# FFN gates in a Mamba and SwiGLU kernel: three Silus in a stretch of their own on ScalarE in place of Tanh and a VectorE operation for each

## What is computed

```python
h = x * rsqrt(mean(x * x) + 1e-05) * norm_w
xs, res = split(h @ in_proj_w.T)                  # 256 channels each
u = silu(causal_conv4(xs) + conv_b)
delta, Bm, Cm = split(u @ x_proj_w.T)             # 64, 16, 16
delta = softplus(delta @ dt_proj_w.T + dt_proj_b)
# state[d, n] = exp(delta * A) * state + delta * u * Bm ; y = sum_n state * Cm, over 512 tokens
y = (y + u * D) * silu(res)
x = layernorm(x + y @ out_proj_w.T + x)
gate, up = x @ wg.T, x @ wu.T                     # 384 hidden units, weights are int / 127
x = layernorm(x + (silu(gate) * up) @ wd.T)
```

## Time and profile before

| | |
|---|---|
| timed runs | 622.06, 623.67, 625.15 us; median 623.67 |
| profiled execution | 623.23 us; span 621.3 us |
| busy | TensorE 442.2 us (71%), VectorE 536.4 (86%), ScalarE 354.9 (57%), GpSimd 388.2 (62%) |
| chain that ended last | VectorE 37%, TensorE 22%, issue 17%, ScalarE 10%, GpSimd 8% |
| TensorE's granted clock, mean | 0.798 of full speed |

### The profile page before, as it was taken

One profiled execution on the slowest core, in us unless ns is written; L12 is line 12 of the kernel. 1 busy time (PEld: TensorE's weight loads), 2 busy tenths in 40 slices (PEclk: granted clock), 3 DMA queues, 4 the chain that ended last, 5 costly groups with the idle time before them and its releaser, 6 DMA issues.

```text
span 621.3 us, 5665 instructions
## 1 busy us (share of the span) xinstructions
PE 442.2 (71%) x1469; PEld 175.7 (28%) x1469; DVE 536.4 (86%) x584; ACT 354.9 (57%) x592; POOL 388.2 (62%) x168
## 2 busy tenths in 40 slices
PE   3963957778859777786958875986958784667443
PEld 2411311323314223322414232422323240312232
DVE  4536999799999899989998899999999999999823
ACT  2264677458653975567753965387556955344322
POOL 4504667854975857865884777676695587575000
PEclk9955968787789879788969879887979887757767
DMA  8038005410246006510443005600533024600000
GB/s 210 0 77 195 1 0 120 102 49 1 36 100 152 2 1 136 125 27 0 90 100 97 0 4 131 152 0 0 135 81 71 0 52 95 141 1 0 17 1 17
DMA packets 27359, 39.10 MB, mean 63 GB/s; under 512 B 3816, under 2 KB 10056, under 8 KB 27344
## 3 DMA queue, kind: packets, MB, share of 16 engines
q1 hardware_dynamic: 25424, 38.51, 27.1%
q10 hardware_dynamic: 1920, 0.42, 0.4%
HBM read 3.27 MB, written 2.10 MB: 9 GB/s over the span
## 4 chain that ended last, share of the span: by engine, by line
DVE 37%; PE 22%; issue 17%; ACT 10%; POOL 8%; SPq 3%; DMA 2%; DVEq 1%; ACTq 0%; POOLq 0%
DVE state L783 18%; DVE weighted L792 11%; POOL prod L649 6%; PE c_ps L386 4%; PE y_ps L397 4%; PE dense_ps L417 3%; SPq L315 3%; ACT decay_ps L504 2%; PE dense_ps L446 2%; PE dense_ps L419 2%; PE dense_ps L452 1%; DMA du_rep<-z_wm 1%; ACT L504 1%; ACT x L515 1%; ACT L539 1%
## 5 line engine op out<-in xcount | busy, mean ns | idle before, releaser
L649 POOL TENSOR_TENSOR prod<-du_rep,b_rep 128x2048 f32<-128x2048 f32 x63 | 284.8, 4530 | 64.7 <-DVE state L783 32.3
L783 DVE TENSOR_TENSOR_SCAN state<-decay_ps,prod 128x512 f32<-128x512 f32 x256 | 299.3, 1207 | 23.0 <-ACT decay_ps L504 10.1
L504 ACT ACTIVATE decay_ps<-delta_rep,a_neg 128x512 f32<-128x512 f32 x256 | 172.2, 686 | 78.6 <-DVE state L783 75.7
L386 PE MATMUL c_ps<-xd,pick 96*128 96x512 f32 x128 | 92.9, 816 | 81.3 <-DVE weighted L792 81.2
L792 DVE TENSOR_TENSOR weighted<-state,c_ps 128x2048 f32<-128x2048 f32 x64 | 146.4, 2287 | 2.7 <-DVE state L783 0.6
L397 PE MATMUL y_ps<-weighted,gather 128*32 128x512 f32 x512 | 93.6, 813 | 5.6 <-DVE weighted L792 5.6
L669 POOL TENSOR_TENSOR rs<-ve,powm 128x4 f32<-128x4 f32 x16 | 16.2, 1012 | 108.0 <-ACT nm L510 108.0
L417 PE MATMUL dense_ps<-h_t,tap_t 128*128 128x512 f32 x128 | 65.3, 658 | 11.8 <-ACT h_t L534 11.8
L386 PEld LDWEIGHTS c_ps<-xd,pick 96*128 96x128 f32 x128 | 27.0, 239 | 115.8 <-DVE weighted L792 104.5
L509 ACT ACTIVATE ve<-mv 128x4 f32<-128x4 f32 x16 | 3.3, 205 | 71.7 <-DVE mv L818 45.9
L417 PEld LDWEIGHTS dense_ps<-h_t,tap_t 128*128 128x128 f32 x128 | 25.4, 209 | 48.3 <-issue 40.1
(11 more groups left out here) (109 smaller groups left out, 538.0 us busy)
## 6 DMA issues: line engine op xcount, KB each, us to landing
delta_rep<-z_ln SPq DMA_DIRECT2D x64, 256.0 KB, 4.7
du_rep<-z_wm SPq DMA_DIRECT2D x64, 256.0 KB, 4.8
out_dram<-y_out SPq DMA_DIRECT2D x8, 256.0 KB, 4.5
state<-L_attn_in_proj_w_in ACTq DMA_DIRECT2D x1, 256.0 KB, 4.2
x_all<-L_attn_x_in SPq DMA_DIRECT2D x1, 256.0 KB, 4.7
weighted<-L_ffn_w_gate_in SPq DMA_DIRECT2D x1, 192.0 KB, 10.6
weighted<-L_ffn_w_up_in SPq DMA_DIRECT2D x1, 192.0 KB, 4.7
weighted<-L_ffn_w_down_in SPq DMA_DIRECT2D x1, 192.0 KB, 5.1
```

The source lines that it names most:

```text
L386: mm(c_ps[:, :], pick[:, CHUNKS + quad % CHUNKS, :], xd[it.now][:, :], start=True, stop=True).then_inc(c_ready, 1)
L504: A(decay_ps[n % DECAYS][:, :], delta_rep[:, h, c, :], ACT.Exp, scale=a_neg[:, col:col + 1]).then_inc(decay_ready, 1)
L649: TT(prod[quad % 2][:, :, :], du_rep[:, h, :, :], b, ALU.mult).then_inc(prod_ready, 1)
L783: dve.tensor_tensor_scan(state[:, n % BLOCKS, :], decay_ps[n % DECAYS][:, :], prod[n // BLOCKS % 2][:, n % BLOCKS, :], 0.0, ALU.mult, ALU. ...
```

## The change

The three Tanhs on ScalarE and the three scalar_tensor_tensors on VectorE go. ScalarE makes the three Silus at step 18, in a loop, directly from PSUM into g_act. z_w and z_wm move from steps 18 and 19 to 19 and 20. TensorE makes the three gates first and the up products behind them, in another order of banks; VectorE multiplies by up at steps 20, 21 and 22 instead of 20, 21 and 23.

```diff
-    SILU2 = WSCALE * WSCALE * WSCALE / 2
+    WSCALE2 = WSCALE * WSCALE
-        g_th = sb("g_th", [P, 2, T])
-        g_th_ready = sem("g_th_ready")
-                ["C", "S", "gate0", "up0", "gate1", "up1", "gate2"],
+                ["C", "S", "gate0", "gate1", "gate2", "up0", "up1"],
-                "gate0": 1, "up0": 2, "gate1": 0, "up1": 1, "gate2": 2, "up2": 0, "b0": 1, "b1": 2,
+                "gate0": 1, "gate1": 2, "gate2": 0, "up0": 1, "up1": 2, "up2": 0, "b0": 1, "b1": 2,
# ScalarE
-                    if step == 18 and it.k0 > -1:
+                    if step == 19 and it.k0 > -1:
                         it.wait(act, z_step, 4, 1, 3)
                         A(z_w[:, :, :], z_e[:, :, :], ACT.Copy, bias=1.0).then_inc(z_step, 1)
-                    if step == 19 and it.k0 > -1:
+                    if step == 20 and it.k0 > -1:
                         it.wait(act, du_in[1], 16 * BLOCKS, 0, 16 * BLOCKS)
                         it.wait(act, z_step, 4, 1, 4)
                         A(z_wm[:, :, :], z_w[:, :, :], ACT.Copy, bias=-1.0).then_inc(wm_ready, 1)
-                    for b, at in enumerate((18, 19, 21)):
-                        if step == at:
+                    if step == 18:
+                        for b in range(HID):
                             it.wait_full(act, f"gate{b}")
-                            A(g_th[:, b % 2, :], it.ps(f"gate{b}")[:, :], ACT.Tanh, scale=WSCALE / 2
-                              ).then_inc(g_th_ready, 1)
+                            it.take(A(g_act[:, b, :], it.ps(f"gate{b}")[:, :], ACT.Silu, scale=WSCALE), f"gate{b}")
# VectorE
-                    for b, (at, then) in enumerate(((19, 20), (20, 21), (22, 23))):
-                        if step == then:
+                    for b, at in enumerate((20, 21, 22)):
+                        if step == at:
                             it.wait_full(dve, f"up{b}")
                             it.wait_taken(dve, f"gate{b}")
                             it.take(TT(g_act[:, b, :], g_act[:, b, :], it.ps(f"up{b}")[:, :], ALU.mult), f"up{b}")
-                    for b, (at, then) in enumerate(((19, 20), (20, 21), (22, 23))):
-                        if step == at:
-                            it.wait(dve, g_th_ready, HID, -1, b + 1)
-                            it.take(STT(out=g_act[:, b, :], in0=g_th[:, b % 2, :], scalar=1.0,
-                                        in1=it.ps(f"gate{b}")[:, :], op0=ALU.add, op1=ALU.mult), f"gate{b}")
-                                    scalar=SILU2, in1=x1[:, 2 * n:2 * n + 2, :],
+                                    scalar=WSCALE2, in1=x1[:, 2 * n:2 * n + 2, :],
```

## The result

The changed kernel takes 639.36 us (median of four, 633.16 to 642.41), the kernel before beside it 624.30: a ratio of 1.023, 95% interval 1.0145 to 1.0324. It is slower, as forecast, but by 15 us and not by 9; 639.36 lies 1.4 us above the range. A second set of six times gave 641.73 (ratio 1.022, 1.017 to 1.027). The ten times fall in two groups: four between 633.2 and 637.1 and six between 641.6 and 643.4. Three of the ten, 633.2 to 634.3 us, lie beside the forecast of 632.5; six lie above the 638 us of the slowest rival but D.

What follows compares the result with a forecast made beforehand. Batch ends were set by when GpSimd can start the next multiply(0), through soften(0) and DMA replication. soften(0) +16.0, hidden -4.0, proj wait -1.75, iteration 7 -0.6, iteration 8 -0.7: about +9, forecast 632.5 us, range 626.5 to 638.

Steps and rivals of the forecast that it cites:

- D: Rival: each table switch costs a drain as well, +15 us on top, 647 us; chance 0.02.
- The chain through z_wm, soften and replication: Late z_wm delays GpSimd's error, multiply(6), soften(0), then replication and the next batch's multiply(0); soften(0) 16.0 us later in all.
- Loads: ScalarE around the gates: 15 more table loads of 1.28 us, the first nearly hidden by the gate0 wait, the second paid.
- The delay of z_wm: ScalarE's z_wm ends 4 to 4.7 us later, making soften(0) 2.25 us later at fast clock, 3.5 us at slow.
- Iterations 1 and 4 are of this sort, 2, 3, 5 and 6 of the first: Gate stretches: two iterations at TensorE's slow clock (soften(0) +3.5 us each), four at the fast clock (+2.25 us each).
- 12.0 less 1.75: Iterations 1 to 6: soften(0) 16.0 us later, 4.0 hidden, leaves 12.0; iteration 4's PE wait for proj gives back 1.75.
- rival C: Slow clock in all gate stretches: 6 x 3.5 - 4.0 - 1.75 - 0.7 = +14.5, 638 us; chance 0.10.
- -0.6 and -0.7: Gains from removed VectorE operations in iteration 7 (0 to -1.3, taken -0.6) and the tail, iteration 8 (-0.7 us).
- it gains 0.3 us there, at the fast clock up to 1.3: VectorE at up2's product: waits 1.5 us, saved 1.8; worth nothing in iterations 1 to 6, real in iteration 7.
- A: Rival: VectorE is the bound, so the removed operations count; some -5 us, 618.5 us; chance 0.09.
- B: Rival: effects cancel within 0.5%, fast gates everywhere and early PE waits absorbing half; +1.7, 625.4 us; chance 0.08.
- E: Rival: Silu comes from the active table set, no loads, soften +1.0 all hidden; chance under 0.01, counted in B.

Runs made afterwards that it cites:

- Experiment 3: Kernel before (Tanh, no loads, old TensorE order) with only z_w at step 20 and z_wm behind the third Tanh at step 21; 652.45 us, ratio 1.044.
- 2: Changed kernel with z_w and z_wm both at step 18, ahead of the three Silus; 641.94 us, ratio 1.027.
- 6: Changed kernel with z_w and z_wm at step 18 ahead of the Silus, and eight unread matmuls ahead of the seventh C; 623.07 us, ratio 0.997.
- profile of 635.1 us: First profiled execution of the unaltered changed kernel, named by its span; the execution took 637.07 us, mean TensorE clock 0.814.
- profile of 640.1 us: Profiled execution from the repeat of the unaltered changed kernel, named by its span; the execution took 642.14 us, clock 0.788; the repeat's median was 641.73 us.
- Version 8: Changed kernel with z_w and z_wm at step 18, the three Silus at step 21, up products at steps 22, 22 and 23; 613.27 us, ratio 0.982.
- experiment 4: Changed kernel with eight extra unread matmuls on TensorE between b1 and the seventh list's C; 632.30 us, ratio 1.012.
- experiment 1: Changed kernel with Tanh in place of the three gate Silus, so no table loads around the gates; 632.16 us, ratio 1.010.
- experiment 10: Version 8 with Ln directly behind the Silus, three table loads per iteration instead of four (u's not counted); 620.93 us, ratio 0.993.

## Why the prediction was right in its direction and wrong in its size

**The chain through z_wm, soften and replication: right.** `multiply(0)` waits for du_rep in iterations 1 to 5 of the profile (in iteration 6 for 0.64 us for a scan). From `soften(0)` to the product the six iterations have 4.0 us less than before in all, the 4.0 that the forecast called hidden. Experiment 3 makes the cost with z_wm alone, experiments 2 and 6 take it away (prod's wait 7.7 and 7.8 us).

**Loads: right.** 15 more, 1.28 us each, the first beside the wait for gate0, the second in full, no drain. The Trainium skill (page ScalarE: Activation LUTs, section What ACT_TABLE_LOAD costs) counts about 1.38 us of drain besides the load for every switch. The rows of the changed kernel don't show it: the load at 225.44 takes 1.28 us, and the decay behind it starts at 226.73.

**The delay of z_wm: near for each clock, wrong for how often.** From the start of the previous `multiply(0)` to `error` the kernel before had 43.0 to 43.2 us in four iterations and 44.8 and 45.6 in two. I added 4.05 to the four and 4.7 to the two: 47.1, and 49.5 and 50.3. Measured are 47.3 to 48.6 in the profile of 635.1 us, and in that of 640.1 49.3 to 49.5 in four iterations and 48.0 and 48.6 in two. The step that failed is the sentence "Iterations 1 and 4 are of this sort, 2, 3, 5 and 6 of the first": it kept the clock of each iteration as it had been, with two slow gate stretches of six. The profile of 635.1 us has two as well (iterations 2 and 4, at 0.59 and 0.66), that of 640.1 us five at 0.56 to 0.59. Forecast for iterations 1 to 6 were 12.0 less 1.75, 10.25 us. The first profile has 419.93 against 409.09, +10.8; the second 426.46, +17.4. In the first `soften(0)` is 14.8 us later in all, in the second 21.6, for a forecast of 16.0 less 1.75. Six of ten executions are in the group of the second. It is also 2 us more than my rival C, with the slow clock in all six, had for this part (21.0 - 4.0 - 1.75 = 15.25). C took 3.5 us for each iteration, which is the delay against a slow iteration of the kernel before. Its iterations 2, 3, 5 and 6 were fast ones, and against them `soften(0)` is 3.6 to 4.5 us later in the profile of 640.1 us.

**Iteration 7: wrong sign; iteration 8: right.** The forecast gave -0.6 and -0.7. From iteration 6's first product to the start of the last weighting the two profiles have +2.6 and +2.1 us, and from there to the end about -0.6 in both. The step that failed is "it gains 0.3 us there, at the fast clock up to 1.3": I followed TensorE to up2 and not on to what it does afterwards. Done early, it idles 6.30 us in iteration 7 before the next C, and C, S and down0 run at 1.2 GHz; r2 waits 2.78 us. Scan 20 waits 1.27 us more for its decay, which I had covered by the longer DMA chain, and iteration 7 has no such chain. I had costed what VectorE gains and nothing for TensorE's clock.

**Iteration 0**, where z_w and z_wm move as well, was left out of the sum; +0.9 in one profile and -0.1 in the other.

**The rivals.** A (VectorE the bound), B (they cancel), D (a drain) and E (no loads) did not come. C (the slow clock in all gate stretches, 638 us) is nearest to the median, though one gate stretch of six in the profile of 640.1 us was at the full clock. VectorE's busy time fell by 12.8 us (536.4 to 523.6), not by the 16 that I had named as a sign, and its idle time grew by 26.6 (84.9 to 111.5). Version 8, without the late z_wm and without the idle time, is 11 us faster than the kernel before. That fits saved operations that count, but no run takes them apart from the rest. The wait of VectorE for decays, 10.1 to 16.9 us, is a cost that I had covered by the DMA chain; where that chain is gone it is on the path, as in 2.

**What stays open.** Which of the two groups an execution falls in was not controlled. That the slow level of the gates' stretch and the idle time of 4.04 us go together in five iterations is seen; which of them brings about the other is not. An idle time of 4.04 us doesn't by itself make the gates of the next iteration slow: behind it they ran at 1.00 in iteration 3 of the first profile and in iteration 4 of the second. Nor is it needed: in experiment 4 the gates of iteration 2 ran at 0.59 without it. Experiments 4 and 6, in which no idle time of 4.04 us is left, have no times 8 us apart. The new order on TensorE with the old gates was not tried, so what the order alone does to the clock is not known. The old order with three Silus in one stretch was not tried either: gate2 waits there for a bank that VectorE frees at step 20, behind a decay that would stand behind the Silus.

## What to carry to other kernels

An operation taken from the busiest engine is worth nothing while that engine waits elsewhere for a chain; ask first what the moved instructions (here two plain copies of z) release, and how many queues and transfers hang on them. Table loads are not dear in themselves: the same six per iteration stand in a kernel of 639 us and in one of 613, depending on whether the work that others wait for was issued ahead of them; in the order of the change the two of the gates cost 7 to 10 us. Before a slower version is put down to an edit, compare TensorE's clock in the same stretch of both, as experiment 10 shows. When TensorE gets its work done earlier, look at how long it is then idle and at what clock it starts the next piece; a job that is early can make the following one late.

## What the runs showed of the hardware that was not expected

After 4.04 us without a matmul in the changed kernel the next two (128x512, 96 rows, fp32) took 2.08 us at a granted clock of 0.50, after 1.33 us in experiment 4 they took 1.13 us, and behind running work in the kernel before 1.02, at 1.00. The length of the idle time alone doesn't decide it: in experiment 1 the same C, at the same place behind 3.53 us of idle time, took 2.08 us in iteration 4 and 1.13 us in iteration 5. Eight matmuls without any use, some 2 us of work, made one kernel 19 us faster (641.94 to 623.07) and another 13 us slower (613.27 to 626.12).
